# Layer 3 of a four-layer kernel: ScalarE rounds the next weight chunk at an earlier place in its program

## The reference, cut to what matters

```python
def _gemma_mlp(x, gate_w, up_w, down_w):          # I = 1024
    g = einsum('bsh,hi->bsi', x, gate_w)
    u = einsum('bsh,hi->bsi', x, up_w)
    return einsum('bsi,ih->bsh', gelu(g, approximate=True) * u, down_w)
out = sum over experts e of dense_w[b, e] * _gemma_mlp(x, gate_e, up_e, down_e)   # two per batch
out = out + _gemma_mlp(x, shared_gate, shared_up, shared_down)
...
att = softmax(q k^T / sqrt(HD)) over the 16 heads of one token
x = x + (att v) @ Wo + bo
x = x + sum_e softmax(h2 @ Wg + bg)_e * (h2 @ We_e)                               # E = 8
```

## Time and profile before

| what | value |
| --- | --- |
| median of 3 runs | 1705.32 us (1702.97 to 1709.03) |
| profiled execution, its own time | 1711.46 us |
| its span | 1709.7 us |
| mean granted TensorE clock | 0.872 of full speed |
| busy: TensorE matmul, weight load | 1348.7 us (79%), 1133.6 us (66%) |
| busy: DVE, GpSimd, ScalarE | 1066.1 (62%), 722.4 (42%), 551.8 us (32%) |
| layer 3 with its MLP | about 946 to 1530 us of the span |

### The profile page before, as it was taken

How to read it: one execution, slowest core, us unless ns; L and a number is a source line. 1 busy time by engine, 2 the same in 40 slices (tenths; PEclk the granted TensorE clock), 3 DMA queues, 4 the chain that set the end, 5 groups by cost and what they waited for, 6 DMA issues and landing times.

```text
span 1709.7 us, 18390 instructions
## 1 busy us (share of the span) xinstructions
PE 1348.7 (79%) x6484; PEld 1133.6 (66%) x6484; DVE 1066.1 (62%) x1879; ACT 551.8 (32%) x872; POOL 722.4 (42%) x342
## 2 busy tenths in 40 slices
PE   5479799999798388835979888987899888976628
PEld 4379678699686387734757676766677667755416
DVE  6149765659764254426866433388658965996984
ACT  2120221310311266621425344433552344332001
POOL 3122011542002555555623334376647564753562
PEclk9759887889696699976989999999999999996858
DMA  7990000220000488852301222212121212200001
GB/s 288 412 412 32 13 25 22 92 85 25 1 0 31 153 240 249 250 163 69 105 25 64 69 103 74 82 67 74 56 80 68 81 63 85 68 13 25 25 19 42
DMA packets 57787, 164.64 MB, mean 96 GB/s; under 512 B 6480, under 2 KB 26208, under 8 KB 57568
## 3 DMA queue, kind: packets, MB, share of 16 engines
q1 hardware_dynamic: 42992, 112.48, 20.4%
q10 hardware_dynamic: 10096, 38.40, 5.7%
q0 software_dynamic: 4608, 12.59, 2.2%
HBM read 109.97 MB, written 53.48 MB: 96 GB/s over the span
## 4 chain that ended last, share of the span: by engine, by line
PE 19%; DVE 16%; POOL 8%; issue 7%; ACT 4%; DMA 0%; DVEq 0%; POOLq 0%; ACTq 0%
PE bank L348 6%; PE bank L352 6%; PE bank L351 6%; POOL w_lo L537 4%; DVE G L370 3%; ACT w_hi L1240 2%; DVE bank L1827 2%; POOL VW L370 2%; DVE acc L1851 2%; DVE F L1851 1%; DVE hid_lo L1781 1%; PE bank L932 1%; DVE acc L1983 1%; DVE G L1765 0%; POOL acc L497 0%
## 5 line engine op out<-in xcount | busy, mean ns | idle before, releaser
L537 POOL TENSOR_TENSOR w_lo<-raw,w_hi 128x1536 fp32r<-128x1536 f32 x48 | 168.7, 3515 | 284.6 <-ACT w_hi L1240 262.5
L348 PE MATMUL bank<-x_hi,w_hi 128*128 128x512 f32 (+1 forms) x560 | 224.6, 401 | 63.1 <-POOL w_lo L537 38.6
L351 PE MATMUL bank<-x_lo,w_hi 128*128 128x512 f32 (+1 forms) x560 | 216.2, 386 | 0.0
L352 PE MATMUL bank<-x_hi,w_lo 128*128 128x512 f32 (+1 forms) x560 | 215.5, 385 | 0.0
L482 POOL TENSOR_TENSOR w_lo<-raw,w_hi 128x1024 fp32r<-128x1024 f32 (+2 forms) x57 | 140.7, 2469 | 121.4 <-ACT w_hi L1086 119.6
L348 PEld LDWEIGHTS bank<-x_hi,w_hi 128*128 128x128 f32 x560 | 112.5, 201 | 95.4 <-POOL w_lo L537 49.2
L348 PE MATMUL bank<-hid_hi,w_hi 128*128 128x512 f32 x328 | 131.9, 402 | 31.3 <-DVE hid_lo L1457 19.6
L479 POOL CAST w_hi<-raw 128x1024 fp32r<-128x1024 f32 (+2 forms) x21 | 23.3, 1110 | 268.0 <-issue 200.2
L351 PE MATMUL bank<-hid_lo,w_hi 128*128 128x512 f32 x328 | 129.9, 396 | 0.0
L352 PE MATMUL bank<-hid_hi,w_lo 128*128 128x512 f32 x328 | 129.5, 395 | 0.0
L352 PEld LDWEIGHTS bank<-x_hi,w_lo 128*128 128x128 f32 x560 | 111.9, 200 | 20.4
(11 more groups left out here) (396 smaller groups left out, 3612.2 us busy)
## 6 DMA issues: line engine op xcount, KB each, us to landing
raw<-in_skill SPq DMA_DIRECT2D x32, 768.0 KB, 4.2
xs<-we_hi ACTq DMA_DIRECT2D x7, 3072.0 KB, 31.5
raw<-in_l1e SPq DMA_DIRECT2D x38, 513.0 KB, 4.5
xs<-we_hi ACTq DMA_DIRECT2D x5, 2560.0 KB, 28.6
raw<-in_shared SPq DMA_DIRECT2D x16, 768.0 KB, 4.2
base<-xs SPq DMA_DIRECT2D x38, 256.0 KB, 3.5
ys<-F SPq DMA_DIRECT2D x38, 256.0 KB, 4.8
K<-in_l3e SPq DMA_DIRECT2D x16, 512.0 KB, 3.5
```

The costliest lines, as they stand in the source:

```text
L348: i = nc.tensor.matmul(out, sh, mh, start=first, stop=False)
L351: nc.tensor.matmul(out, sh, ml, start=False, stop=False)
L352: return nc.tensor.matmul(out, sl, mh, start=False, stop=last)
L537: nc.gpsimd.tensor_tensor(w_lo[n % W3_SLOTS][:], raw[n % 2][:], w_hi[n % W3_SLOTS][:].bitcast(F32), ALU.subtract).then_inc(w_ready.sem, 1)
```

## The change

`dense_hi(n)` is called at the same even slots for the same chunks. In batch 0 it stands ahead of the gelu of the tile, in the batches behind it stands between the gelu and the wait for the gated product, ahead of hid_hi. Before, it stood behind hid_hi. No instruction is added or taken away, and no other engine's program changes.

```diff
                     if 0 <= p < BATCH:
                         finish3_before(p, i, x, y)
+                    next_chunk = i % 2 == 0 and 2 <= n < CHUNKS3 * BATCH
+                    if next_chunk and b == 0:
+                        dense_hi(n)
                     if b < BATCH:
                         act.wait_ge(*g3_ready(0, g + 1))
                         if g >= 2:
@@
                         nc.scalar.activation(gelu3[g % 2], PB[g % 2][0][:], ACT.Gelu_apprx_tanh).then_inc(g3_gelu.sem, 1)
+                        if next_chunk and b > 0:
+                            dense_hi(n)
                         act.wait_ge(*g3_gated(0, g + 1))
                         if g >= HID3:
                             act.wait_ge(*d3_step(0, g + 1 - HID3))
                         elif g == 0:
                             act.wait_ge(*f2_down(PAIRS - 1, 15))
                         nc.scalar.activation(hid_hi[0][:, g % HID3, :], PB[g % 2][1][:], ACT.Copy).then_inc(g3_hi.sem, 1)
-                    if i % 2 == 0 and 2 <= n < CHUNKS3 * BATCH:
-                        dense_hi(n)
                     if 0 <= q < BATCH:
                         attention3_after(q, i)
```

## The result

The changed kernel takes 1720.01 us (median of 5 runs, 1716.24 to 1721.08) against 1705.63 us (median of 5, 1702.97 to 1709.03): a ratio of 1.0081 with a 95% interval of [1.006, 1.0103]. It is slower by some 14 us; forecast was 13 us faster, and the range ended at 1711.

The account below looks back on a forecast made before the run. TensorE, stalled on w_lo, was taken to bound the first batch, DVE and the port shared with GpSimd the sweeps; -15.2 - 3.1 + 1.0 + 1.1 + 3.3 = -12.9 us gave 1692.4 us, range 1680 to 1711.

Parts of the forecast that it names:

- The first batch's 15.2: First batch, chunks 2 to 12: TensorE's stall on w_lo goes, 9.53 to 8.15 us per chunk, gain 15.2 us.
- the head's 3.1: Head of batch 1: TensorE's three waits for w_lo (1.30, 1.02, 0.41 us) and slower restarts vanish, gain 3.1 us.
- I take the first for the forecast: Sweeps of batch 1: DVE's product wins the port by 0.07 us, period 11.1 us; if GpSimd wins, 13.3.
- product 2 at slot 12, "+2.6": Slot 12 of batches 2 and 3: w_lo starts ahead of DVE's product 2 and holds it, loss 2.6 us.
- the lost-edge rival: Sweeps: GpSimd's product takes the port 0.07 us before DVE's request, 2.2 us at seven places, 1708 us; chance 0.30.
- The softmax subtraction: Batch 1: it finds the port free, 1.22 us instead of 3.26; with a DVE wait of 0.5 gone, -2.6 us.
- The net of that slot, -0.6: Slot 20, batch 1: product 8 waits 3.1 us for w_lo, but TensorE's stall on that w_lo goes, net -0.6.
- The -1.1 at tile 3: End of batch 1's sweeps: at tile 3 w_hi no longer stands between ScalarE's root and gelu, -1.1 us.
- a loss of 2.2 recovered at the next head: Slot 20, batch 2: w_lo ahead of product 8 costs 2.2 us, recovered when TensorE stops waiting for w_lo.
- only the first batch counts: Rival: gains and losses behind the first batch cancel, 1687 us; chance 0.12.
- GpSimd's idle time is gained: Rival: each sweep period falls from 10.91 to 10.25 us over 22 chunks, -14.5 us, to 1672.5 us; chance 0.12.
- The first batch's stall: Rival: ScalarE waits at w_hi, so the first batch's stall stays and 15.2 falls to some 3, about 1704; chance 0.04.

Follow-up runs that it names:

- e1: Changed kernel with the move kept only in batch 0, w_hi behind hid_hi again in batches 1 to 3: 1692.28 us, 0.9906 of the kernel before.
- e2: Changed kernel with the move kept only in batches 1 to 3, batch 0 as before the change: 1728.63 us, 1.01 of the kernel before.
- e3: Changed kernel plus a wait: GpSimd's even product starts after DVE's product of the same half step; 1696.13 us, 0.9923 of the kernel before.
- e4: Changed kernel plus a wait: at slot 12 of batches 2 and 3 w_lo starts after DVE's expert gate; 1707.45 us, 0.999 of before.
- e5: Changed kernel plus waits ordering the port: w_lo behind DVE's first product, GpSimd's even product behind DVE's next; 1698.9 us, 0.9941 of before.
- e9: Changed kernel, w_hi behind hid_hi at slots 4 to 19 of batches 2 and 3, port waits in selected places: 1684.42 us, 0.9865 of before.
- e11: Changed kernel plus four 128x2 memsets on GpSimd ahead of each even product, no wait added: 1702.94 us, 0.9971 of the kernel before.
- e7: Changed kernel plus one 128x8 memset on GpSimd ahead of each even product, no wait added: 1715.03 us, 1.0041 of the kernel before.
- e6: Changed kernel with the move kept only in batch 0 and slots 0 to 8 of batch 1, no wait added: 1690.42 us, 0.9897 of before.
- e10: Changed kernel with the two added waits of e3 and e4 together: 1691.58 us, 0.991 of the kernel before.

## Why the prediction was wrong

**What bounds the kernel, and the two gains: right.** The first batch's 15.2 came as 15.1, from chunks 8.16 us apart, and the head's 3.1 as 3.1. e1 keeps the first one to the end, e2 has the second one alone. One thing I had not seen: at the start of the layer the gelu of tile 2 stands behind w_hi by 1.3 us, which the next chunks absorb.

**The step that failed first: "I take the first for the forecast".** The cycle was computed to 0.07 us: GpSimd's product at 4.58 and DVE's request at 4.65 us after a product's start. In the changed kernel the rows stand 0.13, 0.11, 0.09, 0.07 and 0.05 us apart (1120.38, 1133.64, 1171.83, 1185.04 and 1362.24 by DVE's start), always in the order computed, and in all five DVE waited: the rows are 3.33 to 3.41 us long. A sixth race, GpSimd's product 9 ahead of DVE's by 0.10 us at 1165.04, I had not computed; it was lost too (3.36 us). The two arguments for the other outcome were weak. That a waiting product begins 0.14 us before the end of GpSimd's row speaks of how a row ends, not of when the port is taken. And "the rows' starts are not the moments at which the port is taken" was a reason for not knowing, not for one side. The periods, 11.1 won and 13.3 lost, were both right: 11.17 (e3) and 13.26 (the changed kernel). The sweeps of batch 1 came at +10.9. e3, where DVE has each of these edges, has +2.4 there, so losing them cost 8.4 us: 4.2 in the scores and 4.2 at 1165.04 and 1185.04. The one lost at 1171.83 cost nothing of its own, since product 10 meets w_lo there in e3 (1165.15, 3.36 us), as forecast. That e3 ends at -12.7, beside the forecast's -12.9, is luck: 3.4 us of it come from the last attention, which no term had.

What the page SBUF — State Buffer of the Trainium skill says (Who interferes with whom), that whoever issues first keeps the port for the whole instruction, held here down to 0.04 us (the page writes it of DVE's two-port modes; these products have two SBUF inputs, of which it says that they contend). It should have been read strictly: the rival that did so had the right mechanism and the right sign in batch 1.

**The step that failed second: product 2 at slot 12, "+2.6".** I followed w_lo into the slot of DVE's product and overlooked what stands between gated and that product in batches 2 and 3: the gate's instructions (L1930, L1931 before; L1933, L1934 after). They take 0.16 and 0.19 us when free, and I had written that DVE's other instructions run on unhindered, since they have an operand in PSUM or only one. These two have both in SBUF. The term was 5.9 in batch 2 and 6.0 in batch 3, and e4 takes 5.9 and 6.0 of it away with one wait. This is why even the lost-edge rival, 1708, was too low: 3.3 and 3.4 of the missing 12 us.

**The other terms.** The softmax subtraction finds the port free, as forecast (1149.88, 1.23 us instead of 3.26), and gives 2.6 us (-10.81 to -13.42). Slots 14 to 18 of batches 2 and 3 give 1.5 us in each as forecast. w_lo at slot 20 of batch 1 does take the port from product 8, by 0.22 us: the row at 1158.45 is 4.28 us long, a wait of 3.1 as computed. The net of that slot, -0.6, came in e3 (-17.6 to -18.2 from tile 20 to 22), but by luck: "TensorE's stall on that w_lo goes" is wrong, TensorE waits 5.50 us for it where it had waited 5.62, and what went is the wait of product 9 (3.25 us at 1177.08 before, 1.33 in e3). The -1.1 at tile 3 did not come: from tile 23 of batch 1 to tile 4 of batch 2 e3 has +0.3. From tile 20 of batch 2 to tile 4 of batch 3 the shift goes from -1.4 to +2.3, where the forecast had a loss of 2.2 recovered at the next head. It was not all recovered (e3 has +1.6 over the same tiles), and an edge was lost on the way (1362.24), 2.2 us.

**What is left of the miss.** In the trace the layer is 10.8 us longer where -12.9 was forecast, 23.7 us between them. Lost edges are 10.6 of it (8.4 in batch 1, 2.2 in batch 2), the gate 6.7, and two steps of 1.6 us between tiles 10 and 11 of batches 2 and 3 (below), which no step of mine had, 3.2. Another 1.4 is the rest of batch 1 (+2.4 in e3 for +1.0), 1.6 the loss at slot 20 of batch 2 that was not recovered, and 0.2 is left. The rival of the lost edge priced seven of them at 15.4 us; it had the right mechanism, and too many edges made up for part of what it lacked. The medians differ by 14.4 us and the traced executions by 9.1: that of the kernel before lies 5.8 above its median, that of the changed one 0.6.

**The rivals.** That only the first batch counts, and that GpSimd's idle time is gained, both fall with e2. The first batch's stall went. What the gained idle time would need is what e5 and e9 built: the port given in a fixed order. Even then a period is 10.75 and not 10.25.

## What to carry to other kernels

Work made ready earlier starts earlier, and on a shared resource it may then start ahead of something more urgent: before moving a producer, list every instruction of the other engine that shares the port in the slots to which its consumer moves, the tiny ones too, and compare starts. Where two requests come within a few tenths of a microsecond of each other, do not forecast the outcome but fix it with a semaphore: here one wait turned +0.8% into -0.8%. And put such waits only where the order matters: in the last attention the wait for DVE's product of the same slot gained 2.5 us (e3: 3.4 where the changed kernel gives 0.9), and the wait for its next product lost 11 (e5).

## What the runs showed of the hardware

**How near the port's decision is to the start of a row.** Over these runs GpSimd's product ahead of DVE's request by 0.04 us (e2, 1375.66 and 1375.70, DVE's row 3.42 us) and by 0.05, 0.07, 0.09, 0.11 and more kept DVE out each time in the sweeps of layer 3; ahead by 0.03 us (e11, 1113.23 and 1113.26, 1.21 us) or by 0.01 (e7) it did not. In this kernel the decision lies between 0.03 and 0.04 us of difference between the rows' starts, which are given to 0.01 us. The races that DVE won all have memsets directly ahead of GpSimd's product; those lost include some with memsets too, down to 0.04 us. That one is in the last attention (e11): GpSimd's product starts at 1560.34 and the gate's instruction of 128x4 elements at 1560.38, with a row of 2.30 us. With GpSimd 0.17 us ahead there (e1 and the changed kernel) it is 2.17 us long, which is the same wait.

**A waiting instruction gets in between two of GpSimd's.** At 1107.04 DVE asks while w_lo runs (1105.84, 3.50 us). GpSimd's next instruction starts its row without a pause at 1109.31, and the row is 3.39 us long where that product alone takes 2.4: DVE's product got in between. In the rows above DVE waits for one and never for two in a row, so the cost of a lost race is one GpSimd instruction, whether the loser is 1.22 us long or 0.16.

**Small memsets cost less than their rows.** Against DVE's request, one of 0.11 us moved the product behind it by 0.00 to 0.05 us, four of 0.20 us in all by 0.10 to 0.13.

**A step of the clock of fixed size.** Between tiles 10 and 11 of batch 2 the changed kernel loses 1.6 us (-7.37 to -5.73). The view of stretches shows the granted clock (seventh of the columns behind the stretch: busy times of five engines, clock, share of DMA, GB/s), first before, then after:

```profile
1260.00:1265.00 5.00, 5.00 (x37) 4.61 (x36) 3.61 (x4) 3.74 (x4) 1.80 (x1) 1.00 0.32 108
1265.00:1270.00 5.00, 5.00 (x24) 4.27 (x24) 0.00 (x0) 2.15 (x3) 5.00 (x3) 0.69 0.43 146
```

```profile
1251.00:1256.00 5.00, 5.00 (x35) 4.65 (x34) 3.61 (x4) 3.29 (x4) 4.01 (x1) 0.94 0.37 108
1256.00:1261.00 5.00, 5.00 (x20) 4.71 (x21) 0.00 (x0) 1.55 (x2) 4.96 (x3) 0.50 0.49 157
```

TensorE is busy throughout in both, and in the second stretch the clock is at 0.69 before and at 0.50, which is 1.2 of 2.4 GHz, after. The step comes in after and e2 (batches 2 and 3), in e4 and e9 (batch 3 only) and in e7 (batch 2 only), not in e1, e3, e6, e10 and e11, and one of the same size stands in the first batch of e5 and e6. Steps of about that size also go the other way, between tiles 4 and 5: in e10 and e11 in batch 2, in e1 and e6 in batch 3. e10 is the same program as e3 until slot 12 of batch 2, and yet 1.4 us ahead of it at tile 12, so the steps can differ between executions of the same work; the clock is granted at 1.00 in e10 (1203 to 1208 us), at 0.66 in e3 (1204 to 1209 us). They follow none of the edits, so I take them as the clock's own reaction to when the matmuls come; that is not shown, and what sets it off is open and wasn't tried.
